# One block in 32 of a row gather moved from GpSimd to SyncE, row by row with register addresses

## The reference

```
h    = x @ W_in2f
Wij  = (ssp(edge_attr_64 @ Wf1 + bf1) @ Wf2 + bf2) * edge_weight1
m    = segment_sum(h[dst] * Wij, src)          # gather by dst, add by src
m    = ssp(m @ Wo1 + bo1) @ Wo2 + bo2
out  = layernorm(x + (x + m))                   # ssp(v) = softplus(v) - log 2
```

## Time and profile before

| | |
|---|---|
| median of 3 runs | 1828.89 us (1828.09 to 1830.81) |
| the profiled execution | 1837.85 us, of which the profile spans 1836.1 us |
| mean granted TensorE clock | 0.986 |
| first stage | to about 1380 us |
| second stage | from there to the end |

### The profile page before, as it was taken

The page is one execution under the profiler, slowest core; times in us unless marked ns, Lnnn a source line. Parts: engine busy times, 40 slices in busy tenths (PEclk is TensorE's granted clock), DMA queues, the critical chain, the costliest instruction groups (busy, mean ns, idle before and its releaser), DMA issues.

```text
span 1836.1 us, 36487 instructions
## 1 busy us (share of the span) xinstructions
PE 1740.3 (95%) x11376; PEld 1543.6 (84%) x11376; DVE 1507.6 (82%) x3750; ACT 1484.6 (81%) x2945; POOL 1429.4 (78%) x1385
## 2 busy tenths in 40 slices
PE   4989999999999999999999999999978999999995
PEld 3778888888888888888888888888877999999995
DVE  3777877888878888778888788888866999999996
ACT  3777877778787787777787888888757999999996
POOL 5554688888888888888888877777764999999997
PEclk9999999999999999999999999999988999999998
DMA  9999866666666666666666656777655899999994
GB/s 340 373 385 392 218 120 119 114 120 121 115 121 118 119 121 115 122 121 115 121 118 116 119 109 113 155 148 154 127 88 193 288 361 362 360 362 361 362 362 171
DMA packets 177340, 363.45 MB, mean 198 GB/s; under 512 B 25623, under 2 KB 76265, under 8 KB 177149
## 3 DMA queue, kind: packets, MB, share of 16 engines
q1 hardware_dynamic: 101128, 257.75, 40.7%
q0 software_dynamic: 75136, 102.45, 34.0%
q10 hardware_dynamic: 884, 0.92, 0.2%
HBM read 206.90 MB, written 154.12 MB: 197 GB/s over the span
## 4 chain that ended last, share of the span: by engine, by line
PE 23%; POOL 23%; issue 3%; DMA 2%; ACT 1%; DVE 1%; another core or an unknown queue 0%; POOLq 0%; ACTq 0%; DVEq 0%
PE pair L411 15%; POOL sums L387 14%; POOL to_spare L383 5%; PE pair L497 4%; POOL acc L356 2%; PE pair L422 2%; POOL to_spare L381 1%; PE pair L435 1%; PE pair L434 1%; DMA acc<-sums,src_ix 1%; DMA xg<-in_x,dst_t 1%; DVE msg_l L674 0%; ACT zs L584 0%; ACT zs L578 0%; POOL xg L343 0%
## 5 line engine op out<-in xcount | busy, mean ns | idle before, releaser
L356 POOL DMA_INDIRECT acc<-sums,src_ix x392 | 631.9, 1612 | 163.6 <-issue 103.2
L343 POOL DMA_INDIRECT xg<-in_x,dst_t x392 | 394.8, 1007 | 184.8 <-issue 110.3
L387 POOL TENSOR_SCALAR sums<-sums,to_spare 128x256 f32<-128x256 f32 x392 | 283.1, 734 | 10.2
L623 ACT ACTIVATE m_h<-pair,wgt_t 128x256 fp32r<-128x256 f32 x392 | 164.5, 476 | 133.8 <-PE pair L411 98.6
L497 PE MATMUL pair<-m_h,same 128*128 128x256 f32 (+1 forms) x980 | 252.2, 291 | 7.1 <-issue 3.6
L497 PE MATMUL pair<-m_l,same 128*128 128x256 f32 (+1 forms) x980 | 244.8, 284 | 0.0
L411 PE MATMUL pair<-wo_h,msg_h 128*128 128x256 f32 (+1 forms) x784 | 233.5, 298 | 10.7 <-DVE m_l L784 7.3
L497 PEld LDWEIGHTS pair<-m_h,same 128*128 128x128 f32 (+1 forms) x980 | 187.3, 191 | 41.9 <-DVE m_l L784 20.7
L411 PE MATMUL pair<-wo_h,msg_l 128*128 128x256 f32 (+1 forms) x784 | 222.3, 284 | 0.0
L411 PE MATMUL pair<-wo_l,msg_h 128*128 128x256 f32 (+1 forms) x784 | 221.4, 282 | 0.0
L767 DVE SCALAR_TENSOR_TENSOR pair<-pair,bias_w,h_sb 128x512 f32<-128x512 f32 x196 | 147.9, 755 | 89.2 <-PE pair L411 62.2
(11 more groups left out here) (104 smaller groups left out, 5563.2 us busy)
## 6 DMA issues: line engine op xcount, KB each, us to landing
acc<-fill SPq DMA_DIRECT2D x197, 256.0 KB
xg<-in_x SPq DMA_DIRECT2D x97, 512.0 KB
sums<-acc SPq DMA_DIRECT2D x97, 512.0 KB, 6.9
out<-sums SPq DMA_DIRECT2D x97, 512.0 KB, 4.8
attr<-in_edge_attr SPq DMA_DIRECT2D x196, 128.0 KB
srcb<-in_src_rows SPq DMA_DIRECT2D x98, 256.0 KB
xg<-in_x,dst_t POOLq DMA_INDIRECT x392
acc<-sums,src_ix POOLq DMA_INDIRECT x392
```

The source lines that it names most:

```text
L343: pool.indirect_dma_start(xg[0:g.p, g.xs, r], None, t["x"], bass.IndirectOffsetOnAxis(ap=dst_t[0:g.p, r, g.n:g.n + 1], axis=0)).then_inc(x ...
L356: pool.indirect_dma_start(acc, bass.IndirectOffsetOnAxis(ap=src_ix[g.slot][0:g.p, r:r + 1], axis=0), sums[0:g.p, g.slot, r], None, compute ...
L387: last = pool.tensor_scalar(normed[0:g.p, g.n % NRING, r], res[0:g.p, u, r], neg_mean[0:g.p, u, r:r + 1], rstd[0:g.p, u, r:r + 1], ALU.add ...
L623: act.activation(m_h[0:g.p, r], bank[6][0:g.p, k * D:(k + 1) * D], ACT.Copy, scale=col(wgt_t, r, g)).then_inc(mh_sb, 1)
```

## The change

In nine groups (n = 30, 38, ..., 94) the fourth block, r = 3, is no longer gathered by POOL. SP fetches its 128 rows instead, each in a transfer of its own of 1 KB, from an address that SP loads into a register. The host lays out a new DRAM input `dst_rows` (98 x 128, the indices of each group's fourth block side by side). In each of the steps n = 16 to 87, after `load_src` (and the clears, which are over by then), SP calls for 16 addresses of the group m = n - n % 8 + 14 and issues 16 row transfers; so eight steps fetch one block, and the block of group 30 is fetched in steps 16 to 23. PE's `turn_x` of such a group waits, beside the count of the gathers that are left, for 128 landed rows on one of two new semaphores. POOL's counting of gathers (`gathered`) is unchanged: the block that is left out still counts.

```diff
+BY_ROWS = 8
+ROWS_A_STEP = 16
...
+        rows_in = [sem(f"rows_in{u}") for u in range(2)]
...
+        def by_rows(n):
+
+            return AHEAD <= n < G - 1 and (n - XRING + 2) % BY_ROWS == 0
+
         def xg_count(g):
 
-            return sum(16 * R for n in range(g.xs, g.n + 1, XRING))
+            return sum(16 * (R - 1 if by_rows(n) else R) for n in range(g.xs, g.n + 1, XRING))
...
+            def fetch_rows(g, a):
+
+                wait(sp, xt_ps, (g.n - XRING + 1) * 2)
+                _, rows = nc.values_load_multi_w_load_instructions(t["dst_rows"][g.n:g.n + 1, a:a + ROWS_A_STEP], engines=[mybir.EngineType.SP],
+                                                                   min_val=0, max_val=N - 1)
+                for e, row in enumerate(rows, a):
+                    sp.dma_start(xg[e:e + 1, g.xs, R - 1], t["x"][bass.ds(row, 1)]).then_inc(rows_in[g.n // BY_ROWS % 2], 16)
...
                 clear_to(FIRST_CLEARS + (n + 1) * CLEARS_A_STEP)
+                m = n - n % BY_ROWS + XRING - 2
+                if by_rows(m):
+                    fetch_rows(group(m), n % BY_ROWS * ROWS_A_STEP)
                 if G - XRING <= n:
...
                 while gathered < min(count, G * R):
-                    gather(gathered % R)(group(gathered // R))
+                    if gathered % R < R - 1 or not by_rows(gathered // R):
+                        gather(gathered % R)(group(gathered // R))
                     gathered += 1
...
                     pe.wait_ge(xg_in[g.xs], xg_count(g))
+                    if by_rows(g.n):
+                        pe.wait_ge(rows_in[g.n // BY_ROWS % 2], 16 * P * sum(by_rows(n) for n in range(g.n % (2 * BY_ROWS), g.n + 1, 2 * BY_ROWS)))
...
+    laid["dst_rows"] = by_group(inputs["dst"]).transpose(0, 2, 1, 3).reshape(G, R, P)[:, R - 1]
```

## The result

The changed kernel takes 2102.79 us (median of 4 runs, 2098.24 to 2112.47), against 1828.56 us for the kernel before in runs beside it: a ratio of 1.1517, 95% interval 1.1488 to 1.1545, or 274 us more. The forecast of 1827 us was wrong, and so was the range, which ended at 1930. It went the way of the first rival, SP sets the pace, and beyond the prices worked out there (1908 and 2034 us).

What follows compares the result with a forecast made beforehand. PE was taken to bound the first stage, with a small toll from POOL's backlog. Saving 2.0 us, with SP's added work hidden, took the profiled 1836.1 us to 1834.1, and the runs' median of 1828.9 to 1827 us; range 1818 to 1930.

Steps and rivals of the forecast that it cites:

- SP sets the pace: Rival: SP's step exceeds PE's once a row costs over 0.73 us; priced at 1908 and 2034 us; chance 0.33.
- What bounds the kernel: First stage: PE bounds it, at 13.61 us a group while POOL has a backlog and 13.19 after.
- toll: First stage: PE loses 0.42 us a group while POOL's backlog lasts.
- the 2.0 us: Saving from fewer POOL gathers: its backlog ends 4.7 groups earlier, 0.42 us each; bounds 0 and 12.0 us.
- SP's sum: SP's whole work in a step with the change: 12.6 us, fitting under PE's 13.19; ends 8.4 and 60.7 us.
- The issue and its register work: SP, each step: issuing 16 row transfers at 0.47 us, 7.5 us; bounds 6.1 and 11.2 us.
- Register work: SP, each step: address arithmetic, perhaps a bounds test, one gap a row, 0.8 us; bounds none and 3.2 us.
- The address load: SP, each step: 16 addresses from DRAM in one trip, 2.8 us; bounds 0.8 and 44.8 us.
- SP's own work: SP, each step: what it already did before the change, 1.10 + 0.33 us and gaps, 1.5 us.
- A trip for each address: Rival on SP's address loads: each address pays its own trip, step 21.0 us, time 2373 us; chance 0.07.
- 72 d - 18 us: Time lost over 72 steps if SP's step is 13.19 + d us, after about 18 us of slack.
- What would show it: Trace signs: if right, SP still waits for DVE; wrong by SP, DVE's compare waits for srcb in steps 16 to 87.

Runs made afterwards that it cites:

- e3_left_out: Changed kernel, but nobody fetches the fourth block of the nine groups and SP does nothing new: 1832.01 us, 0.9986 of the kernel before.
- e11_half_scatters: Kernel before the change, with only the first and third scatter of each group made: 1809.32 us, 0.9897 of the kernel before.
- e2_fixed_rows: Changed kernel, with the 1152 row transfers from constant addresses, no address load, test or register: 1845.99 us, 1.0054 of the kernel before.
- e1_no_test: Changed kernel without the bounds test on the loaded addresses; loads and row transfers stay: 1868.07 us, 1.0165 of the kernel before.
- e10_late: Changed kernel, with only groups 86 and 94 fetched by rows (SP's steps 72 to 87), bounds test kept: 1882.01 us, 1.0295 of the kernel before.
- e4_three_groups: Changed kernel, with only groups 30, 38 and 46 fetched by rows (SP's steps 16 to 39): 1920.29 us, 1.046 of the kernel before.
- e5_addresses_only: Changed kernel, with SP loading and testing addresses but issuing no row transfers, POOL gathering every block: 1857.74 us, 1.011 of the kernel before.
- e7_sbuf_no_test: Changed kernel without the bounds test, SP's registers loaded from a small table in SBUF instead of DRAM: 1865.17 us, 1.0153 of the kernel before.
- e12_half_no_test: e1_no_test with only the first and third scatter of each group made: 1823.21 us, 0.9974 of the kernel before.
- e6_one_transfer: Changed kernel, with one transfer of 16 neighbouring rows at a constant address replacing each sixteen: 1834.26 us, 0.9987 of the kernel before.

## Why the prediction was wrong

**What bounds the kernel** was read rightly: PE, with a toll while POOL has a backlog. The toll was explained by the backlog's length and not by POOL's time; e3_left_out, with about 2.6 us for nine gathers, agrees with the 2.0 us but does not tell them from none. That the toll goes with the backlog is borne out: with half of the scatters 18.6 us came back (e11_half_scatters), and PE's excess in steps 14 to 74 is 3.5 us, against 27.0 in the kernel before.

**The failed step is SP's sum**, "7.5 + 0.8 + 2.8 + 1.5 = 12.6 us a step, against 13.19". It measures 17.47. By terms:

- The issue and its register work, 7.5 and what the gap of 0.05 stood for: 7.33 measured. A little below the estimate; with constant addresses the same 16 issues take 4.80 (e2_fixed_rows).
- "Register work", 0.8 us with 3.2 as the upper bound, held the bounds test in a half sentence. The test alone took 4.56 us, above its own upper bound. The nearest row was a gap between two transfers, and 32 added instructions can't be priced by a gap. This term is most of the error, 3.8 us of 4.9 if the whole 0.8 is set against it, and without it nine tenths of the loss are gone (e1_no_test).
- The address load, 2.8: 3.77 measured. "One trip a step" was wrong; it is two, one behind the other, since the table's own address is loaded first.
- SP's own work, 1.5: 1.82.

The upper end given for a step, 60.7 us, held the truth, but the chance on it (0.33 for SP sets the pace, ended at 1930 in the range) came from three terms each taken near its lower end. With a bar of 0.6 us in 13.19 and three terms that no row showed, the likelier side was the other one.

**A trip for each address** did not happen: 16 indices come in about 2.1 us together, the pointer in 1.6 on average. The rule of the Trainium skill, Runtime: NRT & Kernel Launch, section Instruction fetch mechanics, about 200 ns a register, would give an estimated 3.2 us for the 16; the trace shows less for these (2.1), and 3.77 with the pointer that the sum by the page left out. The floor of about 600 ns in the Trainium skill, DMA: Bandwidth & Descriptors, section Latency and other measured facts, is not paid once for each register here: 16 x 0.6 would be an estimated 9.6 us, and the 16 took 2.1.

**The price "72 d - 18 us"** held: with d = 17.47 - 13.19 = 4.28 it gives 290 us, and PE's excess in the trace of the changed kernel adds up to 291.7. The slack measured 15.4 (e10_late) and 16.6 us (e4_three_groups), and the toll that the kernel before pays until it has caught up, 27 us in its profiled execution, is no longer paid, since PE waits for SP in any case: 308 - 16 - 27 = 265, or 279 with a toll of 13 as in e10_late, against 274 measured.

**What would show it** was right in its wrong-by-SP half: the compare waits for `srcb` in each step, SP waits for DVE once for 0.3 us in 612, PE's pace is SP's step. The wait of `fetch_rows`, which was never to hold, held four times for 2.6 us together in that window; PE's new wait, for landed rows, does not show there.

**Not foreseen by any rival** is the second cost, 1.1 to 1.7% of the whole time, paid while POOL is behind: it appears with SP early (e5_addresses_only, e7_sbuf_no_test) and ends with POOL's backlog (e12_half_no_test). It is 1.1% for loads and tests, 1.5% for loads and transfers. Whether the 0.5% for sixteen transfers with constant addresses (e2_fixed_rows, against -0.1% for one in e6_one_transfer) is the same cost is not shown, since its trace has no excess over the kernel before. The second cost would probably have decided the sign even if the step of 12.6 us had been right, as it did in e7_sbuf_no_test. That it needs both, SP's many small instructions and POOL's backlog of indirect transfers, is shown; what the two share is not, and stays open.

## What to carry to other kernels

Before work is put on an engine that looks idle, count the instructions that one line of the program becomes: a load of addresses brought a load of the table's pointer and two instructions of bounds test for each index, and without the test, which the source shows only as a minimum and a maximum, nine tenths of the loss are gone. When a time has to stay under a bar, no single term is the culprit: the transfers alone fitted, the address work alone fitted, and their sum did not. Let the sum decide only if it stays below the bar with its unseen terms at their upper ends; 0.6 us of 13.19 was no margin. And ask what an engine's idle time sits beside: the same instructions on SP were free once POOL had worked off its backlog and cost about 0.8 us a step before (e1_no_test, 33.6 us more than the kernel before in steps 14 to 59).

## What the runs showed of the hardware

- A load of 16 adjacent indices from DRAM into SP's registers took 2.1 us, behind a load of the table's pointer of 1.6 us (2.0 in the step shown); from SBUF the 16 took 1.21 us in all.
- A bounds test of one index took 0.25 us on SP, longer than the 0.22 us of issuing a row.
- A transfer of one row of 1 KB follows the next after 0.30 us with a constant address and 0.41 us with a register's; 16 rows in one transfer took 0.43 us to issue.
- SP's small instructions show pauses. A register instruction of a row transfer is usually followed by the next instruction after less than 0.1 us. In e1_no_test 98 of 772 are followed only after more than 0.35 us between 490 and 840 us, with POOL behind (0.6 us on average), and 22 of 514 between 1000 and 1215 us, with POOL caught up. In e12_half_no_test, where POOL has caught up, it is 23 of 852 between 490 and 840 us. So SP, too, is disturbed while POOL works off its backlog; by what, is not shown.
